# Softmax attention with fp32r row tiles, 1024 wide exponentials and a ring of single maximum banks

## Chip, cores and metric

The kernel runs on one core of a Trainium2 chip. The metric is device time in microseconds (us) of one execution. PE is TensorE (PEld its weight loads), ACT ScalarE, DVE VectorE, POOL GpSimd, SP SyncE.

## What is computed

4096 tokens of 256 features pass a linear attention with a layer norm, then a transformer block: layer norm, 16-head softmax attention (head width 16) with an output projection, and a mixture of 8 experts with the best 2 taken. The change is in the softmax attention and what touches it.

```python
h = _layernorm(x, ln1_g, ln1_b)
q = (h @ Wq).reshape(Bb, Ss, H, Dh)
k = (h @ Wk).reshape(Bb, Ss, H, Dh)
v = (h @ Wv).reshape(Bb, Ss, H, Dh)
scores = jnp.einsum('bqhd,bkhd->bhqk', q, k) / jnp.sqrt(jnp.float32(Dh))
attn = jax.nn.softmax(scores, axis=-1)
ctx = jnp.einsum('bhqk,bkhd->bqhd', attn, v).reshape(Bb, Ss, Dd)
x = x + ctx @ Wo
```

The results have to be close to fp32, so operands of fast matmuls are split into parts.

## The kernel before

`linear_attention` ends with a loop over 8 chunks of 512 tokens (`project`, `split`): Q, K and V are projected in fp32, and Q, K and the difference of two K halves (`k_diff`) are split into three bf16 parts by ACT (L325, L331) and DVE (L423, L435) and stored to DRAM by SP.

`softmax_attention` runs 16 heads x 8 query chunks = 128 chunks. Every chunk has 16 steps, of 2 x 128 keys each. Scores are computed transposed (keys on partitions, 512 queries in the free dimension), as one matmul of 96 rows of parts and 2 rows that subtract the row maximum (`scores`, L683). So the maximum must be known before a chunk's scores: it is found 7 chunks ahead. `diff_unit` (L627) computes q(k1 - k2), ACT takes the Relu (L728), `b_unit` (L636) computes qk2, and one DVE instruction (L797) adds the two and takes the maximum. `finish_max` (L773, L775) makes the two rows, and SP writes them into `q_ring` with two DMAs (`rows`, L534), each from 4 partitions to one.

ACT takes two 512 wide exponentials a step (L741). The low part of each probability is made by DVE in 11 steps of 16 (L804) and by POOL in 5 (L590). `values` (L666) multiplies high and low parts with three parts of V in two column halves of the array, five steps later (`LAG`). ACT copies the sum (L733), PE turns it with fp32 matmuls (L649), DVE divides it. Every engine executes its instructions in the order of its own program and waits for the others on semaphores.

Seven chunks of maxima run before the first scores. `output_projection` collects the heads, turns them, multiplies with Wo and adds x1.

The order of PE in a step is the core of the matter:

```python
scores(t, 0)
if ahead:
    diff_unit(n, t)
scores(t, 1)
if ahead:
    b_unit(n, t)
values(i, par if t >= LAG else par_before, t - LAG)
```

## Time and profile before

| | before |
|---|---|
| median of 3 runs | 4782.31 us (4779.12 to 4784.58) |
| the profiled execution, its own time | 4777.63 us |
| its span | 4775.8 us |
| mean granted TensorE clock | 0.942 |
| busy: PE, DVE, ACT, POOL | 4253.5, 3625.5, 3703.7, 2061.1 us |
| DMA | 176.13 MB |

Busy time is the time in which an engine had an instruction in flight. "Idle before" is the time that it stood before a group's instructions, with the instruction that ended the wait. PEclk is the granted clock as a share of 2.4 GHz. An fp32 matmul is recorded as two.

### The profile page before, as it was taken

How to read it: one execution, taken by the hardware profiler on the slowest of the kernel's cores; microseconds unless marked ns; L12 is line 12 of the kernel's file. 1: busy time of each engine (PE TensorE's matmuls, PEld its weight loads, DVE VectorE, ACT ScalarE, POOL GpSimd, SP SyncE). 2: the span in 40 equal slices, each digit the busy share in tenths (PEclk: the TensorE clock that was granted, in tenths of full speed). 3: DMA queues.
4: the chain of work that ended last, by engine and by line, in shares of the span. 5: the costliest groups of instructions: out<-in, count | busy, mean ns of one | idle time of the engine just before them, and what ended most of it. 6: DMA issues, size and time to landing. Idle time of an engine off the chain costs nothing. (4 is left out here: it accounts for less than half of the span.)

```text
span 4775.8 us, 95820 instructions
## 1 busy us (share of the span) xinstructions
PE 4253.5 (89%) x22137; PEld 1697.9 (36%) x22137; DVE 3625.5 (76%) x7256; ACT 3703.7 (78%) x6958; POOL 2061.1 (43%) x1018
## 2 busy tenths in 40 slices
PE   7569999999999999999999999999999963499991
PEld 4322222222222222222222222222222243499991
DVE  3658898989899889988898998889898863133335
ACT  1347999999999999999999999999999841255551
POOL 0011343434344443434343443434343423788875
PEclk8777999999999999999999999999999985699995
DMA  2231010101001010101011010101010014334433
GB/s 78 101 83 17 0 17 0 17 0 17 5 12 17 0 17 0 17 0 17 0 17 16 2 17 0 17 0 17 0 17 0 0 51 140 123 138 137 137 115 114
DMA packets 105461, 176.13 MB, mean 37 GB/s; under 512 B 16512, under 2 KB 87552, under 8 KB 99072
## 3 DMA queue, kind: packets, MB, share of 16 engines
q1 hardware_dynamic: 86864, 146.17, 11.9%
q0 software_dynamic: 6336, 16.79, 1.1%
q10 hardware_dynamic: 12144, 12.06, 0.7%
q14 instruction: 99, 0.81, 0.1%
q8 instruction: 18, 0.29, 0.0%
HBM read 117.55 MB, written 57.15 MB: 37 GB/s over the span
## 5 line engine op out<-in xcount | busy, mean ns | idle before, releaser
L741 ACT ACTIVATE probs<-s_ps 128x512 f32<-128x512 f32 x4096 | 2430.6, 601 | 213.5 <-PE s_ps L683 161.3
L590 POOL TENSOR_TENSOR probs_low<-probs 128x1024 f16<-128x1024 f32 x640 | 1324.6, 2070 | 2082.9 <-ACT probs L741 2082.9
L804 DVE TENSOR_TENSOR probs_low<-probs 128x1024 f16<-128x1024 f32 x1408 | 1820.5, 1295 | 20.9 <-ACT probs L741 20.7
L797 DVE CUSTOM_DVE_ANT_0 excess<-b_ps,excess 128x512 f32<-128x512 f32 x2048 | 1401.9, 687 | 332.5 <-ACT excess L728 264.7
L683 PE MATMUL s_ps<-q_ring,k_ring 98*128 (+1 forms) x4096 | 1565.1, 384 | 13.8 <-ACT probs L741 8.6
L728 ACT ACTIVATE excess<-diff_ps 128x512 f32<-128x512 f32 x2048 | 1215.4, 594 | 57.9 <-PE diff_ps L627 48.9
L666 PE MATMUL o_ps<-probs,v_parts 128*64 128x512 bf16 x4106 | 854.1, 412 | 74.8 <-ACT o_here L733 72.2
L683 PEld LDWEIGHTS s_ps<-q_ring,k_ring 98*128 98x128 bf16 x4096 | 434.3, 106 | 1160.3 <-ACT probs L741 574.1
L627 PE MATMUL diff_ps<-kd_ring,q_ring 96*128 (+1 forms) x2048 | 801.1, 391 | 50.5 <-issue 38.2
L636 PE MATMUL b_ps<-k_ring,q_ring 96*128 (+1 forms) x2048 | 798.9, 390 | 11.5 <-DVE unit_max L797 10.7
L666 PE MATMUL o_ps<-probs_low,v_parts 128*64 128x512 f16 x4106 | 783.7, 378 | 0.0
L666 PEld LDWEIGHTS o_ps<-probs,v_parts 128*64 128x64 bf16 x4106 | 228.3, 106 | 908.2 <-issue 510.6
L1480 DVE TENSOR_TENSOR hidden_low<-h_ps,hidden_high 128x512 fp32r<-128x512 f32 x184 | 127.2, 691 | 369.8 <-ACT hidden_high L1444 369.8
L1440 ACT ACTIVATE h_ps<-h_ps,b_here 128x512 f32<-128x512 f32 x184 | 121.4, 660 | 261.1 <-PE h_ps L1377 261.0
L636 PEld LDWEIGHTS b_ps<-k_ring,q_ring 96*128 (+1 forms) x2048 | 200.6, 98 | 128.4 <-DVE unit_max L797 61.4
L627 PEld LDWEIGHTS diff_ps<-kd_ring,q_ring 96*128 (+1 forms) x2048 | 201.4, 98 | 98.8 <-issue 93.1
L666 PEld LDWEIGHTS o_ps<-probs_low,v_parts 128*64 128x64 bf16 x4106 | 233.6, 109 | 0.3
L649 PEld LDWEIGHTS misc_ps<-gather,o_here 128*128 128x128 f32 x1032 | 153.2, 188 | 216.4 <-issue 215.2
L1389 PE MATMUL y_ps<-w_low,hidden_high 128*128 128x256 f32 x736 | 209.3, 284 | 0.0
L1389 PE MATMUL y_ps<-w_high,hidden_high 128*128 128x256 f32 x736 | 207.9, 282 | 0.0
L1389 PE MATMUL y_ps<-w_high,hidden_low 128*128 128x256 f32 x736 | 206.7, 281 | 0.0
L649 PE MATMUL misc_ps<-gather,o_here 128*128 128x17 f32 x1032 | 203.6, 273 | 0.7 <-ACT o_here L733 0.7
(195 smaller groups left out, 3445.3 us busy)
## 6 DMA issues: line engine op xcount, KB each, us to landing
w_in<-in_W SPq DMA_DIRECT2D x46, 1024.0 KB, 4.9
q_ring<-qs_dram SPq DMA_DIRECT2D x96, 128.0 KB, 4.4
k_ring<-ks_dram SPq DMA_DIRECT2D x96, 128.0 KB, 7.1
slots_dram<-zero_rows SPq DMA_DIRECT2D x24, 512.0 KB, 6.4
rows_e<-slots_dram SPq DMA_DIRECT2D x24, 512.0 KB, 3.9
y_slots_dram<-y_out ACTq DMA_DIRECT2D x23, 512.0 KB, 4.1
qs_dram<-parts SPq DMA_DIRECT2D x16, 384.0 KB, 3.0
ks_dram<-parts SPq DMA_DIRECT2D x16, 384.0 KB, 4.2
```

What stands on the lines that cost most here:

```text
L590: nc.gpsimd.tensor_tensor(probs_low[:, t % BUFS, :, :], probs[:, t % BUFS, :, :], high[:, :, :, 1], ALU.subtract).then_inc(pool_low_done, 1)
L627: nc.tensor.matmul(diff_ps[:, u % 2, :], q_ring[0:SROWS, ds(q, P)], kd_ring[:, ds(k, CHUNK)], start=True, stop=True).then_inc(diff_done, 1)
L636: nc.tensor.matmul(b_ps[:, u % 2, :], q_ring[0:SROWS, ds(q, P)], keys[:, :, 1, :], start=True, stop=True).then_inc(b_done, 1)
L649: last = nc.tensor.matmul(out_ps[:, t, :], o_here[:, P * t:P * t + P], gather[:, :], start=True, stop=True)
L666: last = nc.tensor.matmul(o_ps[V_COLS * k:V_COLS * k + V_COLS, :], v_parts[:, par, 2 * at + k, :], part[:, k, :], start=(t == 0 and low == ...
L683: nc.tensor.matmul(s2_ps[:, k, :], k_ring[:, col:col + P], q, start=True, stop=True).then_inc(s2_done, 1)
L728: nc.scalar.activation(excess[:, u % 2, :], diff_ps[:, u % 2, :], ACT.Relu).then_inc(excess_ready, 1)
L741: nc.scalar.activation(probs[:, t % BUFS, k, :], s2_ps[:, k, :], ACT.Exp).then_inc(exp_done, 1)
L797: nc.vector.tensor_tensor_reduce(excess[:, u % 2, :], b_ps[:, u % 2, :], excess[:, u % 2, :], 1.0, LEAST, ALU.add, ALU.max, unit_max[:, u ...
L804: nc.vector.tensor_tensor(probs_low[:, t % BUFS, :, :], probs[:, t % BUFS, :, :], high[:, :, :, 1], ALU.subtract).then_inc(low_done, 1)
L1389: last = nc.tensor.matmul(y_ps[:, b, t // 2, D * (t % 2):D * (t % 2) + D], h[:, f % 4, cols], w[:, b, f, :], start=(f == 0 and n == 0 and ...
L1480: nc.vector.tensor_tensor(hidden_low[:, f % 4, :], h_ps[:, f % 2, :], hidden_high[:, f % 4, :].bitcast(F32), ALU.subtract).then_inc(low_do ...
```

## The change

Q and K are split into two fp32r parts in place of three bf16 ones, so a product needs 3 x 16 = 48 rows (50 with the maximum's two). The operands are held twice, at partitions 0 and 64, and two matmuls for two halves of the keys stand side by side in the rows of the array. A slot has one exponential of 1024 columns over both (`s_ps` has two buffers of two banks). Maxima are found two chunks ahead (`LEAD`): in 11 of 16 slots DVE reads both maximum banks by itself, in the 5 of `RELU_PAIRS` the old way with Relu is taken. The maximum banks are a ring of three, `m_ps`, each freed by itself; the turned output takes a turn in it. `finish_max` has four steps, in slots 1, 4, 7 and 10 of the next chunk's maxima, the last a DVE transpose of 32 x 32 blocks, from which SP writes the rows with 16 DMAs (2 row halves x 2 parts x 4 blocks) instead of 2. Probabilities are kept for 16 slots. Five slots of 16 (`FULL_UNITS`) are multiplied in fp32 without a split; the other 11 are split by POOL alone. The visits of P times V stand at the slots of `SLOTS` (those from 16 on fall into the next chunk). Q comes by chunk into four buffers (6 DMAs each); the context goes to DRAM undivided with its sums, two DMAs a chunk, and `output_projection` reads it back, spreads the inverted sums with a matmul per half and scales. The diff, cut to its core:

```diff
-PARTS = 3
...
-Q_PARTS = (0, 0, 0, 1, 1, 2)
-K_PARTS = (0, 1, 2, 0, 1, 0)
...
+PARTS = 2
+Q_PARTS = (0, 0, 1)
+K_PARTS = (0, 1, 0)
...
+TOP_ROW = 64
...
+SIDE = TOKENS // 2
+UNITS = SIDE // P
+KCH = SIDE // CHUNK
+PAIR = 2 * CHUNKS
+RING = HEADS * CHUNKS
+Q_BUFS = 4
+LEAD = 2
+SQ = 32
...
-LAG = 5
-BUFS = 8
...
+ROW_DMAS = 16 * 2 * MROWS * (P // SQ)
+
+FULL_UNITS = (3, 6, 9, 12, 15)
+POOL_UNITS = tuple(t for t in range(UNITS) if t not in FULL_UNITS)
+VISITS = ((0, 1), (3,), (2, 4), (6,), (5, 7), (9,), (8, 10), (12,), (11, 13), (15,), (14,))
+SLOTS = (10, 12, 14, 15, 16, 18, 19, 20, 22, 23, 24)
+COPY_SLOT, TURN_SLOT = 8, 11
+RELU_PAIRS = (1, 4, 7, 10, 14)
+FINISH_SLOTS = (1, 4, 7, 10)
+RING_BLOCKS = 2 * UNITS + 1
+TURN_BLOCK = 2 * TURN_SLOT + 2
...
-                for s in range(5):
-                    act.wait_ge(rest_ready, c * 5 + (s + 6))
-                    nc.scalar.activation(parts[:, b, s, 1, :], rest[:, s, :], ACT.Copy).then_inc(mid_ready, 1)
...
+        q_stage = sb("q_stage", [TOP_ROW + AROWS, Q_BUFS * CHUNK], F32R)
+        k_ring = sb("k_ring", [TOP_ROW + AROWS, 2, SIDE], F32R)
+        kd_ring = sb("kd_ring", [SROWS, 2, SIDE], F32R)
...
+        probs = sb("probs", [P, UNITS, 2, CHUNK])
+        probs_low = sb("probs_low", [P, len(POOL_UNITS), 2, CHUNK], F16)
...
+        excess = sb("excess", [P, CHUNK])
...
+        s_ps = ps("s_ps", [P, 2, 2, CHUNK])
+        m_ps = ps("m_ps", [P, 3, CHUNK])
...
+            def load_q(h, qc, buf):
+                for at in (0, TOP_ROW):
+                    for n, part in enumerate(Q_PARTS):
+                        sp.dma_start(q_stage[at + DH * n:at + DH * n + DH, ds(buf * CHUNK, CHUNK)].bitcast(F32),
...
-                for r in range(MROWS):
-                    sp.dma_start(q_ring[SROWS + r:SROWS + r + 1, ds(col, CHUNK)].rearrange("a (t n) -> a t n", t=TPC),
-                                 max_parts[:, r, :]).then_inc(row_in, 16)
-                sp.wait_ge(row_in, n * (MROWS * 16) + MROWS * 16)
...
+            def rows(n, buf):
+                sp.wait_ge(max_ready, n + 1)
+                for at in (0, TOP_ROW):
+                    for r in range(MROWS):
+                        row = q_stage[at + SROWS + r:at + SROWS + r + 1, ds(buf * CHUNK, CHUNK)].bitcast(F32)
+                        row = row.rearrange("a (t b n) -> a t b n", t=TPC, b=P // SQ)
+                        for b in range(P // SQ):
+                            sp.dma_start(row[:, :, b, :], max_turned[SQ * b:SQ * b + TPC, r, :]).then_inc(rows_in, 16)
...
+                i = sp.snap(h * CHUNKS + qc)
+                if loads:
+                    sp.wait_ge(s_done, i * UNITS + 1)
+                    n = qc + LEAD + 1
+                    load_q(sp.snap(h + n // CHUNKS), n % CHUNKS, n % Q_BUFS)
+                    if more and qc == 0:
+                        load_head(sp.snap(h + 1), sp.snap((h + 1) & 1))
+                if ahead:
+                    rows(i + 1, (qc + 1) % Q_BUFS)
+                if before:
+                    store(i - 1, 1 - qc % 2, sp.snap(h - 1) if qc == 0 else h, (qc - 1) % CHUNKS)
...
+            def max_pair(it, c, t):
+
+                par, buf = c % PAIR // CHUNKS, c % Q_BUFS
+                col = buf * CHUNK + P * (t // KCH)
+                key = CHUNK * (t % KCH)
+                for k, at in enumerate((0, TOP_ROW)):
+                    b = block_of(t, k)
+                    if c * RING_BLOCKS + b > 2:
+                        pe.wait_ge(m_read, it * (PAIR * RING_BLOCKS) + (c * RING_BLOCKS + b - 2))
+                    ring = kd_ring if k == 0 and t in RELU_PAIRS else k_ring
+                    nc.tensor.matmul(m_ps[:, b % 3, :], q_stage[at:at + SROWS, col:col + P],
+                                     ring[at:at + SROWS, par, key:key + CHUNK], start=True, stop=True).then_inc(m_done, 1)
...
+            def scores(it, c, t):
+                par, buf = c % PAIR // CHUNKS, c % Q_BUFS
+                if c * UNITS + t > 1:
+                    pe.wait_ge(exp_done, it * (PAIR * UNITS) + (c * UNITS + t - 1))
+                for k, at in enumerate((0, TOP_ROW)):
+                    last = nc.tensor.matmul(s_ps[:, t % 2, k, :], k_ring[at:at + AROWS, par, P * t:P * t + P],
+                                            q_stage[at:at + AROWS, buf * CHUNK:buf * CHUNK + CHUNK], start=True, stop=True)
...
+                    if t in FULL_UNITS:
+                        for k in range(2):
+                            last = nc.tensor.matmul(o_ps[V_COLS * k:V_COLS * k + V_COLS, :],
+                                                    v_full[:, par, FULL_UNITS.index(t), k, :], probs[:, t, k, :],
+                                                    start=False, stop=False)
+                        continue
+                    for n, part in enumerate((high_view[:, t, :, :, 1], probs_low[:, POOL_UNITS.index(t), :, :])):
+                        for k in range(2):
+                            last = nc.tensor.matmul(o_ps[V_COLS * k:V_COLS * k + V_COLS, :],
+                                                    v_parts[:, par, first_tile(t) + 2 * k, :], part[:, k, :],
+                                                    start=(first and n == 0), stop=(final and n == 1))
...
+            def turn_o(it, c):
+
+                pe.wait_ge(o_copied, it * PAIR + c)
+                pe.wait_ge(m_read, it * (PAIR * RING_BLOCKS) + ((c + LEAD) * RING_BLOCKS + TURN_BLOCK - 2))
+                nc.tensor.matmul(m_ps[:, TURN_BLOCK % 3, :], gather[:, :], o_here[:, :], start=True, stop=True
+                                 ).then_inc(o_turned, 1)
...
+                pe.wait_ge(rows_in, (it * PAIR + (c + 1)) * ROW_DMAS)
+                for t in range(UNITS):
+                    scores(it, c, t)
                     if ahead:
...
+                        max_pair(it, c + LEAD, t)
+                    for visit, slot in enumerate(SLOTS):
+                        if slot == t:
+                            values(it, c, visit)
+                        if slot == t + UNITS and c > 0:
+                            values(it, c - 1, visit)
+                    if t == TURN_SLOT and c > 0:
+                        turn_o(it, c)
...
+            def chunk(i, ahead, first=False):
+                for t in range(UNITS):
+                    if ahead and t in RELU_PAIRS:
+                        excess_pair(i + LEAD, t)
+                    act.wait_ge(s_done, i * UNITS + (t + 1))
+                    if not first:
+                        act.wait_ge(pv_done, i * len(VISITS) + (visit_of(t) + 1 - len(VISITS)))
+                    nc.scalar.activation(probs[:, t, :, :], s_ps[:, t % 2, :, :], ACT.Exp).then_inc(exp_done, 1)
+                    if t == COPY_SLOT and not first:
+                        copy_o(i)
...
+            def pair(n, t, b, skip):
+
+                qt, j = t // KCH, t % KCH
+                if t in RELU_PAIRS:
+                    dve.wait_ge(excess_ready, n * len(RELU_PAIRS) + (RELU_PAIRS.index(t) + 1))
+                    dve.wait_ge(m_done, n * (2 * UNITS) + (2 * t + 2))
+                    dve.sem_inc(dve_passed, 1)
+                    nc.vector.tensor_tensor_reduce(excess[:, :], m_ps[:, block_of(t, 1) % 3, :], excess[:, :], 1.0, LEAST,
+                                                   ALU.add, ALU.max, unit_max[:, b, qt, 2 * j:2 * j + 1]
+                                                   ).then_inc(m_read, 2)
+                    return
+                for k in range(2):
+                    dve.wait_ge(m_done, n * (2 * UNITS) + (2 * t + k + 1))
+                    nc.vector.tensor_reduce(unit_max[:, b, qt, 2 * j + k:2 * j + k + 1], m_ps[:, block_of(t, k) % 3, :],
+                                            AX.X, ALU.max).then_inc(m_read, 1 + skip * k)
...
+                if step == 3:
+                    dve.wait_ge(low_done, n + 1)
+                    nc.vector.transpose(max_turned[:, :, :].rearrange("p r n -> p (r n)"),
+                                        max_parts[:, :, :].bitcast(F32).rearrange("p r n -> p (r n)")).then_inc(max_ready, 1)
...
+            def chunk(n, b, ahead=True, finish=True, turn=True, stores=None):
+
+                for t in range(UNITS):
                     if ahead:
-                        unit(n, t)
-                    if t == LAG + TPC + 3:
-                        finish_max(n)
...
+            def spread(c):
+
+                if c == 0:
+                    pe.wait_ge(z_ready, 1)
+                    pe.wait_ge(picks_made, CHUNKS)
+                if c >= 2:
+                    pe.wait_ge(headsT_ready, 2 * (c - 1))
+                for j in range(HALVES):
+                    heads = of_head[:, c, HEADS // 2 * j:HEADS // 2 * j + HEADS // 2, :].rearrange("p h d -> p (h d)")
+                    last = nc.tensor.matmul(z_ps[:, c % 2, j, :], heads, z_inv[:, :], start=True, stop=True)
...
+            def scale(c):
...
+                for j in range(HALVES):
+                    nc.vector.tensor_tensor(headsT[:, c % 2, j, :], ctxT[:, c, j, :], z_ps[:, c % 2, j, :], ALU.mult
```

## Rows read from the trace of the kernel before

**Rows 1.** Busy time of each engine in a stretch of the main loop (sum 1200 us).

```profile
2400.00:3600.00 1200.00, 1163.55 (x6071) 342.47 (x6069) 1080.67 (x2124) 1131.92 (x2171) 513.66 (x251) 1.00 0.07 9
```

**Rows 2.** The costliest groups of instructions: busy us, mean ns, idle before and releaser.

```profile
L741 ACT ACTIVATE probs<-s_ps 128x512 f32<-128x512 f32 x4096 | 2430.6, 601 | 213.5 <-PE s_ps L683 161.3
L804 DVE TENSOR_TENSOR probs_low<-probs 128x1024 f16<-128x1024 f32 x1408 | 1820.5, 1295 | 20.9 <-ACT probs L741 20.7
...
L1429 ACT ACTIVATE m_high<-mT_e 128x1024 fp32r<-128x1024 f32 x24 | 25.4, 1059 | 0.8
```

**Rows 3.** Single lines of the attention stage: ns min/median/max, first and last start.

```profile
L733 ACT ACTIVATE o_here<-o_ps x19: 592/592/592, 441.1 to 929.3; 128x512 f32<-128x512 f32 x19
...
L741 ACT ACTIVATE probs<-s_ps x4096: 589/597/645, 429.3 to 3859.6; 128x512 f32<-128x512 f32 x196
...
L797 DVE CUSTOM_DVE_ANT_0 excess<-b_ps,excess x2048: 675/685/693, 326.9 to 3713.1; 128x512 f32<-128x512 f32 x187
```

**Rows 4.** Timeline of one chunk: start us, us, engine, line, operation, operands.

```profile
1500.06 0.60 ACT L741 ACTIVATE probs<-s_ps 128x512 f32<-128x512 f32 x1 [0.16 <-PE s_ps L683]
...
1500.08 0.38 PE L683 MATMUL s_ps<-q_ring,k_ring 98*128 x1
...
1500.55 0.59 ACT L728 ACTIVATE excess<-diff_ps 128x512 f32<-128x512 f32 x1
...
1500.60 0.42 PE L666 MATMUL o_ps<-probs,v_parts 128*64 128x512 bf16 x2
...
1500.86 0.38 PE L666 MATMUL o_ps<-probs_low,v_parts 128*64 128x512 f16 x2
...
1501.03 0.60 ACT L741 ACTIVATE probs<-s_ps 128x512 f32<-128x512 f32 x1
...
1501.16 0.40 PE L649 MATMUL misc_ps<-gather,o_here 128*128 128x17 f32 x2
...
1503.09 0.69 DVE L797 CUSTOM_DVE_ANT_0 excess<-b_ps,excess 128x512 f32<-128x512 f32 x1 [1.05 <-ACT excess L728]
...
1503.71 0.08 DVE L797 DVE_READ_ACCUMULATOR2_ANT unit_max<- 128x1 f32 x1
```

**Rows 5.** The POOL split line: ns min/median/max, first and last start.

```profile
L590 POOL TENSOR_TENSOR probs_low<-probs x640: 1892/1895/2875, 439.2 to 3860.4; 128x1024 f16<-128x1024 f32 x160
```

**Rows 6.** SyncE's queue: DMA instructions of two lines, their wait, two in time.

```profile
L534 SPq DMA_DIRECT2D q_ring<-max_parts x270: 595/607/791, 332.3 to 3858.6; - x135
...
L520 SPq DMA_DIRECT2D q_ring<-qs_dram x96: 324/325/953, 302.5 to 3481.3; - x96
...
SPq L537 <- DMA q_ring<-max_parts: 128.9, 135, 1.6
...
1513.43 1.35 SPq L534 DMA_DIRECT2D q_ring<-max_parts  x2
```

**Rows 7.** Stretches of the first phase: busy us of PE, PEld, DVE, ACT, POOL, then PEclk.

```profile
242.00:245.00 3.00, 0.00 (x0) 0.00 (x0) 3.00 (x8) 2.93 (x6) 0.00 (x0) 1.00 0.00 0
245.00:246.00 1.00, 0.82 (x6) 0.82 (x7) 1.00 (x3) 0.30 (x1) 0.00 (x0) 0.82 0.00 0
246.00:249.00 3.00, 3.00 (x10) 2.55 (x9) 2.13 (x4) 1.93 (x3) 0.00 (x0) 0.50 0.75 247
249.00:252.00 3.00, 3.00 (x9) 1.54 (x9) 0.00 (x0) 1.16 (x2) 0.00 (x0) 0.99 1.02 328
```

**Rows 8.** Timeline: fp32 and fp32r matmuls of 512 columns.

```profile
249.52 7.03 PE L270 MATMUL banks<-hT,w_qkv 128*128 128x512 f32 x16
...
4201.13 0.39 PE L1377 MATMUL h_ps<-m_high,w_high 128*128 128x512 f32 x1
...
4201.36 0.40 PE L1377 MATMUL h_ps<-m_low,w_high 128*128 128x512 f32 x1
```

**Rows 9.** Timeline: first instruction of the projection and of the stage behind it.

```profile
3865.93 0.43 SPq L868 DMA_DIRECT2D w_o<-in_Wo  x1
...
3930.98 0.38 SPq L970 DMA_DIRECT2D w_g<-in_Wg  x1
```

More of the change, by code:

```diff
@@ new lines, in _, with chunk @@
+            for i in range(LEAD + 1):
+                load_q(sp.snap(0), i, i)
+            rows(0, 0)
+            def chunk(h, qc, loads=True, more=True, ahead=True, before=True):
+                i = sp.snap(h * CHUNKS + qc)
[9 more added lines that the diff above has]
+                    store(i - 1, 1 - qc % 2, sp.snap(h - 1) if qc == 0 else h, (qc - 1) % CHUNKS)
@@ new lines, in _ @@
+            for qc in range(CHUNKS):
+                chunk(sp.snap(0), qc, before=qc > 0)
+            with sp.Fori(1, HEADS - 1) as h:
+                for qc in range(CHUNKS):
+                    chunk(h, qc)
+            for qc in range(CHUNKS):
+                chunk(sp.snap(HEADS - 1), qc, loads=qc + LEAD + 1 < CHUNKS, more=False, ahead=qc + 1 < CHUNKS)
+            store(RING - 1, 1, sp.snap(HEADS - 1), CHUNKS - 1)
+            for b in range(2):
+                sp.wait_ge(ctx_out[b], 32 * (RING // 2))
@@ L719, in _ @@
+            turn_o(HEADS // 2 - 1, PAIR)
         @block.scalar
@@ L752, in _ @@
+            for n in range(LEAD):
+                for t in RELU_PAIRS:
+                    excess_pair(n, t)
+            chunk(0, True, first=True)
+            with act.Fori(1, RING - LEAD) as i:
+                chunk(i, True)
+            for i in range(RING - LEAD, RING):
+                chunk(i, False)
             copy_o(RING)
@@ L830, in row_statistics @@
+            chunk(RING + 2, 0, ahead=False, finish=False, stores=RING // 2 - 1)
 def row_statistics(nc, dve, ch, stats, mean_var, std, rstd, var_ready, std_ready, n):
```

631 lines of the change are left out of this document (267 added, 364 removed).

## The prediction

> **What bounds the kernel now.** I read the busy time by stretches first, then the groups of instructions, then the timeline of one chunk, and last SyncE's queue. In the main loop [rows 1] ACT is busy 1131.92 of 1200 us, PE 1163.55, DVE 1080.67 and POOL 513.66, at the full granted clock: no engine stands out, POOL is free. Per chunk ACT has 32 exponentials of 512 columns, 16 Relus and a copy [rows 2]; DVE has 11 splits of 1.295 us and 16 fused sums with a maximum, POOL 5 splits. A chunk takes (929.3 - 441.1) / 18 = 27.1 us [rows 3]. The first exponential starts at 429.3 us, and the copy after the last chunk belongs to the projection's start at 3865.9 [rows 3, 9]; the loop with its short last chunks is about 3434 us. What surrounds it is 4777.6 - 3434 = 1344 us of the profiled execution's own time. The median of the three runs is 4.7 us above that time, so the sum needs no correction.
>
> **The engines' sums per chunk after the change.** ACT: 16 exponentials 1024 wide, 5 Relus, a copy. Instructions of 512 columns start 0.49 and 0.48 us apart [rows 4]. A 1024 wide exponential is not in the trace; from below it costs 0.49, from above twice that. The nearest row, a 1024 wide copy at 1059 ns [rows 2] against 601, adds 0.46: I take 0.94 from start to start and 1.04 to its semaphore. Sum 16 x 0.94 + 6 x 0.49 = 18.0 us. DVE: all splits go; 22 single maxima of 512 columns and 5 fused ones. A maximum alone isn't in the trace; the fused one frees DVE after 1503.71 - 1503.09 = 0.62 us and its result is out at 0.70 [rows 4]. Below, 0.49 (ACT's pass over the same 512), above, 0.70; I take 0.62: 27 x 0.62, a copy of 0.62 and 0.8 for the small steps give 18.2 us. POOL: 11 splits, which take 1.895 us where DVE leaves POOL alone and up to 2.875 where not [rows 5]; DVE now reads at most one SBUF tensor. 11 x 1.895 = 20.8 us and per head one split of V (about 7 us, from below 0, from above 11) give 21.7 us a chunk.
> PE: a slot has four fp32r matmuls in two pairs on separate row halves. fp32r of 512 columns starts every 0.23 us [rows 8]. That a row pair runs together is not in the trace; column pairs do, 0.26 us from pair to pair [rows 4]. Below 0.21, above 0.47 a pair; the column pair is nearest, 0.26. An fp32 matmul of 512 columns is 16 records in 7.03 us, two to each, so 0.88 us [rows 8]; I take 0.86 for a full unit's column pair (above 1.72 if its halves run one after the other). From the last column pair to the next matmul 0.30 instead of 0.22 pass [rows 4]: 0.1 us for each change of tiling. 16 x 0.52 + 11 x 0.48 + 5 x 0.86 + 11 visits x 0.2 + 1.0 for the turn = 21.1 us.
> The Trainium skill (TensorE: Matmul & The Clock Gate, Part 3, "Measured speedup vs the span model") has row tiles side by side, 3.07 times for four; by it the pair is as I take it, and no row here shows it. If pairs of fp32r did not overlap, PE would have 16 x 2 x 0.21 = 6.7 us more.
> By sums alone a chunk would take about 22 us. Two things that the sums leave out decide.
>
> **The slots are chained.** The ring of three maximum banks and the single `excess` put PE, ACT and DVE in a row. At a Relu pair the Relu stands ahead of the exponential on ACT and needs the bank that PE fills after its scores; the fused maximum follows it, and frees both banks; the next slot's second maximum matmul waits for that, and the P times V visit is queued behind it. Walked with the durations above: scores of slot 0 at 0, exponential 0 from 0.45 to 1.5, visit ends 1.7; slot 1's bank full at 2.4, Relu to 3.0, maximum to 3.7; slot 2's second bank only then, its visit to 5.0; slot 3 starts at 5.0, slot 4 at 6.7, slot 6 at 9.6, slot 8 at 12.65, slot 10 at 14.45, its Relu behind copy and exponential 9 to 16.3, fused maximum and the fourth finishing step to 17.1 us. On that pace 16 slots take 23.6 us.
>
> **The rows come late.** `finish_max` of chunk i+1 ends after DVE's slot 10 of chunk i. Only then may SP issue that chunk's rows: 2 row halves x 2 parts x 4 blocks = 16 DMAs in place of 2, and PE waits for all 16 ahead of the first scores of chunk i+1. A DMA from four partitions occupies SP for 607 ns, never under 595, where loads of 16 partitions take 325 [rows 6]; two with their address steps take 1.35 us [rows 6], so the gap is from 0 to 0.14; the new addresses are constants, I take 0.05. 16 x 0.607 + 15 x 0.05 = 10.5 us. SP then waited 128.9 us in 135 waits, 0.95 us each, for the rows to land [rows 6]. The other 8 DMAs a chunk (6 loads of Q, 2 stores), and 9 more at a head's start, take 3 to 6 us of SP before slot 10 or after the rows and cost nothing.
> With the walk: 17.1 + 10.5 + 1.0 = 28.6 us, against slots done at 23.6: PE idles about 5 us in each chunk. After an idle stretch of over 3 us the granted clock is 0.82 and then 0.50 (1.2 GHz) over the next 3 us and 0.99 after that [rows 7]. At 1.2 GHz slots 0 and 1 take PE 1.1 and 0.4 us longer (matmuls of 512 columns 0.43 apart instead of 0.22), slot 3 starts at 6.5 and the walk ends 1.5 us later, at 18.6. The period is 18.6 + 10.5 + 0.95 = **30.0 us**, 2.9 more than 27.1.
>
> **The rest.** Before the loop 7 chunks of maxima alone from 326.9 to 429.3 [rows 3] become two, the second up to slot 10, and the first rows: loads until about 320, 20 + 13.5 us of maxima, 11.5 of rows, first exponential at 365: -64 us. In the first phase five copies and five subtractions a chunk go; there PE waits for the normalised rows, which they don't hold up: -5 (0 to -16). DRAM writes grow from 1.9 to 2.5 MB a chunk, beside 16 us of matmuls: 0. The projection took 3930.98 - 3865.93 = 65 us [rows 9]; its transposes and copies are replaced by two fp32 spreading matmuls, PE about 5.2 instead of 5.8 us a chunk, and x1 comes in pieces: -13. The tail after the last exponential (visits, turn, store): +8. Last two chunks without maxima: -15. Sum: 4777.6 - 3434 - 89 + 128 x P = 1254 + 128 P. With P = 30.0: **5100 us**. No change is P = 27.5.
>
> **Rivals.**
> 1. *The walk stalls too much* (faster). If PE, ACT and DVE overlap up to the longest sum, the end of slot 10 is PE's 12.5 us for slots 0 to 9 plus scores, Relu, maximum and step, 14.3 us. P = 25.8, 4550 us; 24.8 to 27.3 over the bounds. It decides from slot 10's end under 16.0 us. For it: before, PE, ACT and DVE run at 90 to 97% of the loop [rows 1]. Against: there DVE and ACT had two buffers each. 25%.
> 2. *The small DMAs are cheap* (faster). At the 325 ns of the loads, 16 take 6 us, rows land by 24.1 us, and the free pace of 23.6 holds, over POOL's 21.7: 4275 us (4030 to 4400). For it: constant addresses. Against: all 270 of this kind took 595 ns or more [rows 6]. 13%. The Trainium skill (DMA: Bandwidth & Descriptors, "Anatomy of one DMA") puts a sequencer's dispatch at some 50 ns; by it 16 would take 0.8 us and this rival would hold; the 607 ns row speaks against it for SP's occupancy.
> 3. *The clock stays at 1.2 GHz* through most of a chunk, or pairs don't overlap. PE then needs 2 x 18 + 2.2 = 38 us a chunk; 33 to 40 by its share: 5480 to 6370, middle 5900 us. For it: idle then dense and sparse slots. Against: at half the clock PE is never idle, and in rows 7 it came back. 13%.
> The forecast (rows late, chained slots) has 47%, with P from 28 to 32.5 and **4840 to 5420 us as its own range**; 2% lie within 0.2% (about 10 us, what a measurement of this kernel can tell from no change). Faster 0.25 + 0.13 = 0.38, slower 0.47 + 0.13 = 0.60. From 4300 to 5550 us leaves out about two thirds of rival 2 and of rival 3, and the ends of the others: 2 in 10.
>
> **What the profile after would show.** Right: about 30 us between the copies of O; SP's row DMAs near 607 ns, 16 in a run of 10 us; PE's wait at a chunk's first scores put down to those DMAs, about 5 us, 126 times, and a clock under full speed behind it; POOL idle several us a chunk; first exponential near 365 us. Wrong: no such wait (rival 2, or a slot pace over 1.9 us), DVE's fourth finishing step less than 16 us after the chunk's start (rival 1), or a clock near 0.5 through whole chunks (rival 3).

## The result, and the profile after

The changed kernel takes 5608.96 us (median of 4 runs, 5577.70 to 5611.69) against 4783.10 us before: ratio 1.1716, interval 1.1679 to 1.1752, so 17% slower. The forecast of 5100 us had the sign and the beginning of the mechanism (rows late, PE idle, clock down), but it was 509 us too low and its range ended at 5550: what the low clock costs was put far too small. The profiled execution took 5611.69 us, its span is 5609.8 us; the terms below are held against that. One of the four executions of experiment e13 took 9637.6 us where the others took 4469.8 to 4473.0; it stands outside that kernel's ratio.

The same stretch of the loop as in [rows 1], by engine:

```profile
core 0: us, PE busy (x) PEld busy (x) DVE busy (x) ACT busy (x) POOL busy (x), PEclk, DMA share, GB/s
2400.00:3600.00 1200.00, 1039.49 (x4576) 394.31 (x4574) 650.36 (x1302) 666.24 (x774) 751.76 (x428) 0.80 0.06 12
```

ACT went from 1131.92 to 666.24 us and DVE from 1080.67 to 650.36. Part of that is only that fewer chunks fit into the stretch: by the chunk (27.1 us before, 34.1 here, see below) ACT went from 25.6 to 18.9 us, DVE from 24.4 to 18.5 and POOL from 11.6 to 21.4, where the forecast had 18.0, 18.2 and 21.7. So the work did move as it was to. PE is still busy 1039 of 1200 us, but at a mean clock of 0.80 where it had 1.00. The steps of 1 us below show the clock at 1.00 or 0.50 but for the steps in which it changes; so a mean of 0.80 is 40% of the time at 0.50.

The copies of O, one a chunk, and SP's row DMAs (groups by tile; ns minimum, median, maximum, then first and last start in us):

```profile
L752 ACT ACTIVATE o_here<-o_ps x128: 592/598/601, 413.8 to 4705.6; 128x512 f32<-128x512 f32 x128
...
L540 SPq DMA_DIRECT2D q_stage<-max_turned x2048: 572/573/771, 356.9 to 4670.5; - x187
```

A chunk takes (4705.6 - 413.8) / 127 = 33.8 us. That mean has the two short chunks at the end in it, which find no maxima; in the middle of the loop the median from one chunk's first scores to the next's is 34.1 us. Before it was 27.1 [rows 3], and 30.0 was forecast.

The costliest groups of the page after, to set beside [rows 2] and [rows 5]:

```profile
L623 POOL TENSOR_TENSOR probs_low<-probs 128x1024 f16<-128x1024 f32 x1408 | 2639.4, 1895 | 1646.9 <-ACT probs L761 1641.3
L761 ACT ACTIVATE probs<-s_ps 128x1024 f32<-128x1024 f32 x2048 | 2071.7, 1024 | 1200.2 <-PE s_ps L673 1197.2
L795 DVE TENSOR_REDUCE unit_max<-m_ps 128x1 f32<-128x512 f32 x2816 | 1810.6, 684 | 1119.0 <-PE m_ps L665 1111.0
L673 PE MATMUL s_ps<-q_stage,k_ring 50*128 50x512 f32 x4096 | 1183.6, 561 | 397.5 <-DMA q_stage<-max_turned 359.9
L789 DVE CUSTOM_DVE_ANT_0 excess<-m_ps,excess 128x512 f32<-128x512 f32 x640 | 442.7, 692 | 874.7 <-ACT excess L748 555.9
```

Every unit price was near its forecast: POOL's split 1895 ns, the 1024 wide exponential 1024, the single maximum 684. ACT, DVE and POOL each wait for something over 1000 us. The fourth row has what they wait for in the end: the scores, and before these the rows.

The timeline from slot 10's maximum to the next chunk's first scores and the transpose after that:

```profile
1508.40 0.69 DVE L789 CUSTOM_DVE_ANT_0 excess<-m_ps,excess 128x512 f32<-128x512 f32 x1 [0.35 <-ACT excess L748]
1509.02 0.24 DVE L822 STREAM_TRANSPOSE max_turned<-max_parts 128x64 f32<-128x64 f32 x1
...
1509.28 9.86 SPq L540 DMA_DIRECT2D q_stage<-max_turned  x16
...
1520.27 0.79 PE L673 MATMUL s_ps<-q_stage,k_ring 50*128 50x512 f32 x2 [3.10 <-DMA q_stage<-max_turned]
...
1543.13 0.24 DVE L822 STREAM_TRANSPOSE max_turned<-max_parts 128x64 f32<-128x64 f32 x1
```

SP starts the 16 DMAs 0.02 us after the transpose ends and is busy 9.86 us with them; PE starts 1.13 us after that, idle for 3.10 us. From the first scores at 1520.27 to the end of the next transpose at 1543.37 pass 23.1 us, where the forecast had 18.6. 23.1 + 9.9 + 1.1 = 34.1 us for this chunk.

The same time in steps of 1 us (columns as above):

```profile
1517.00:1518.00 1.00, 0.16 (x2) 0.00 (x0) 0.47 (x1) 0.07 (x1) 0.87 (x1) 1.00 0.01 1
1518.00:1519.00 1.00, 0.00 (x0) 0.00 (x0) 0.00 (x0) 0.00 (x0) 0.00 (x0) 0.96 0.01 1
1519.00:1520.00 1.00, 0.00 (x0) 0.00 (x0) 0.00 (x0) 0.00 (x0) 0.00 (x0) 0.50 0.01 1
...
1525.00:1526.00 1.00, 0.34 (x1) 0.00 (x0) 0.61 (x1) 1.00 (x3) 0.00 (x0) 0.50 0.00 0
1526.00:1527.00 1.00, 0.85 (x3) 0.42 (x5) 0.81 (x5) 0.95 (x2) 0.89 (x1) 0.50 0.00 0
...
1531.00:1532.00 1.00, 1.00 (x6) 0.23 (x4) 0.32 (x1) 0.00 (x0) 0.00 (x0) 0.50 0.00 0
1532.00:1533.00 1.00, 1.00 (x6) 0.47 (x8) 0.00 (x0) 0.11 (x1) 0.00 (x0) 0.71 0.00 0
1533.00:1534.00 1.00, 1.00 (x6) 0.21 (x3) 0.24 (x1) 1.00 (x2) 0.00 (x0) 1.00 0.00 0
```

The clock falls to 0.50 (1.2 GHz) in the idle stretch and stays there until past 1532, through twelve us after PE has started again. The three waits of PE that matter here:

```profile
PE s_ps L673 <- DMA q_stage<-max_turned: 359.9, 115, 4.9
PE m_ps L665 <- DVE unit_max L789: 106.6, 138, 1.2
PE m_ps L665 <- DVE unit_max L795: 81.2, 261, 0.5
```

So 3.1 us of waiting for the rows in a chunk, 360 us in all, is what the waits show. The larger cost stands in no wait for the rows: it is in the longer slots (experiment e2 sizes it).

### The profile page after: what moved, and what is told of

It is laid out like the page before. It is cut to its first block and busy times, and to the rows that moved or that the text cites. A ratio compares the mean times of both kernels' runs of the same rounds, so it can differ in the third digit from the quotient of the medians.

```text
span 5609.8 us, 80903 instructions
## 1 busy us (share of the span) xinstructions
PE 4634.8 (83%) x21172; PEld 2130.2 (38%) x21172; DVE 2798.5 (50%) x5778; ACT 2805.7 (50%) x3421; POOL 3362.4 (60%) x1877
## 5 line engine op out<-in xcount | busy, mean ns | idle before, releaser
L623 POOL TENSOR_TENSOR probs_low<-probs 128x1024 f16<-128x1024 f32 x1408 | 2639.4, 1895 | 1646.9 <-ACT probs L761 1641.3
L761 ACT ACTIVATE probs<-s_ps 128x1024 f32<-128x1024 f32 x2048 | 2071.7, 1024 | 1200.2 <-PE s_ps L673 1197.2
L795 DVE TENSOR_REDUCE unit_max<-m_ps 128x1 f32<-128x512 f32 x2816 | 1810.6, 684 | 1119.0 <-PE m_ps L665 1111.0
L673 PE MATMUL s_ps<-q_stage,k_ring 50*128 50x512 f32 x4096 | 1183.6, 561 | 397.5 <-DMA q_stage<-max_turned 359.9
L665 PE MATMUL m_ps<-k_ring,q_stage 48*128 48x512 f32 x3456 | 1273.5, 491 | 213.4 <-DVE unit_max L789 106.6
L673 PEld LDWEIGHTS s_ps<-q_stage,k_ring 50*128 50x128 f32 x4096 | 459.0, 218 | 1562.5 <-issue 1217.6
L789 DVE CUSTOM_DVE_ANT_0 excess<-m_ps,excess 128x512 f32<-128x512 f32 x640 | 442.7, 692 | 874.7 <-ACT excess L748 555.9
L665 PEld LDWEIGHTS m_ps<-k_ring,q_stage 48*128 48x128 f32 x3456 | 625.9, 226 | 614.9 <-DVE unit_max L789 307.3
L690 PE MATMUL o_ps<-probs,v_full 128*64 128x512 f32 x2560 | 803.1, 710 | 0.0
L748 ACT ACTIVATE excess<-m_ps 128x512 f32<-128x512 f32 x640 | 380.8, 595 | 752.3 <-PE m_ps L665 751.9
```

The source lines that it names most:

```text
L623: nc.gpsimd.tensor_tensor(probs_low[:, POOL_UNITS.index(t), :, :], probs[:, t, :, :], high_view[:, t, :, :, 1], ALU.subtract).then_inc(poo ...
L665: nc.tensor.matmul(m_ps[:, b % 3, :], q_stage[at:at + SROWS, col:col + P], ring[at:at + SROWS, par, key:key + CHUNK], start=True, stop=Tru ...
L673: last = nc.tensor.matmul(s_ps[:, t % 2, k, :], k_ring[at:at + AROWS, par, P * t:P * t + P], q_stage[at:at + AROWS, buf * CHUNK:buf * CHUN ...
L690: last = nc.tensor.matmul(o_ps[V_COLS * k:V_COLS * k + V_COLS, :], v_full[:, par, FULL_UNITS.index(t), k, :], probs[:, t, k, :], start=Fal ...
L748: nc.scalar.activation(excess[:, :], m_ps[:, block_of(t, 0) % 3, :], ACT.Relu).then_inc(excess_ready, 1)
L761: nc.scalar.activation(probs[:, t, :, :], s_ps[:, t % 2, :, :], ACT.Exp).then_inc(exp_done, 1)
```

## Experiments

The theory was: rows late, PE idle, clock down, slots longer, rows late again. Rival A: the clock falls because the slots are too sparse, wait or no wait. Rival B: the ring of maximum banks with its Relus sets the pace whatever the clock does. The table has, for the profiled run of each kernel, the mean time from copy of O to copy of O over the whole loop, the mean granted clock from 1600 to 2800 us, and PE's waits for the row DMAs divided by 127 chunks; then the median time of the kernel's executions. Each ratio is to the kernel before, measured beside it: median 4783.1 us beside the changed kernel, 4773.0 to 4774.4 beside the experiments that have a ratio. "One run" is a single execution.

| kernel | us a chunk | clock | row wait, us | time, us | ratio to before |
|---|---|---|---|---|---|
| changed kernel | 33.8 | 0.80 | 2.8 | 5609.0 | 1.1716 (1.1679 to 1.1752) |
| e1 steps at slots 0 to 3 | 27.1 | 0.96 | 0 | 4756.0 | 0.9968 (0.9953 to 0.9983) |
| e2 PE kept busy, rows late | 30.8 | 0.98 | 0 | 5222.6 | one run |
| e3 e1, visits in groups | 27.6 | 0.95 | 0 | 4803.1 | 1.0066 (1.0049 to 1.0083) |
| e4 e1, Relu behind | 31.7 | 0.90 | 0 | 5338.0 | 1.1193 (1.1172 to 1.1214) |
| e5 steps at 1, 3, 5, 7 | 27.0 | 0.96 | 0 | 4736.1 | one run |
| e6 e1, no Relu pairs | 26.9 | 0.96 | 0 | 4710.2 | 0.9862 (0.9845 to 0.9879) |
| e7 no Relu pairs, late | 33.6 | 0.83 | 2.6 | 5570.3 | one run |
| e8 last step after slot 9 | 30.4 | 0.91 | 1.9 | 5168.7 | one run |
| e9 e1, steps as reductions | 27.3 | 0.95 | 0 | 4762.4 | 0.9971 (0.9959 to 0.9983) |
| e10 e9, 15 visits | 26.9 | 0.97 | 0 | 4721.0 | 0.9883 (0.9865 to 0.9901) |
| e11 e10, no Relu pairs | 23.9 | 0.99 | 0 | 4331.6 | 0.9081 (0.9066 to 0.9096) |
| e12 e11, late | 30.8 | 0.83 | 3.0 | 5213.0 | one run |
| e13 e9, no Relu pairs | 25.0 | 0.99 | 0 | 4472.2 | 0.9366 (0.9347 to 0.9384) |
| e14 e13, late | 31.4 | 0.86 | 3.0 | 5294.3 | one run |

**e1: the rows in time.** The only edit:

```diff
-FINISH_SLOTS = (1, 4, 7, 10)
+FINISH_SLOTS = (0, 1, 2, 3)
```

> The changed kernel with the four finishing steps of the row maxima after slots 0 to 3 instead of 1, 4, 7, 10; nothing else moved. Theory (rows land late, PE idles about 3 us, the clock falls, the walk to slot 10 runs at half clock, and so the rows are late again): SP starts the 16 DMAs by 8 us of a chunk, they are in by 19 us, no wait for rows, granted clock above 0.95, chunk 23.6 to 25 us, 4280 to 4450 us in all. Rival A (the clock falls without any wait, because the slots of narrow fp32r tiles are too sparse): no wait for rows, but the clock stays near 0.8 and a chunk takes 29 us or more, 4950 us up. Rival B (the ring of maximum banks, Relu and fused maximum alone set the pace): clock above 0.95 and still 28 us or more, 4850 us up.

The loop's stretch (columns as above), then the first scores of two chunks in a row, between which the clock is full:

```profile
1600.00:2800.00 1200.00, 1114.38 (x5674) 428.66 (x5674) 828.50 (x1613) 825.85 (x960) 932.00 (x534) 0.96 0.08 15
```

```profile
1532.32 0.50 PE L673 MATMUL s_ps<-q_stage,k_ring 50*128 50x512 f32 x2
...
1558.63 0.50 PE L673 MATMUL s_ps<-q_stage,k_ring 50*128 50x512 f32 x2
```

853 us came back and rival A fell: with no wait for rows the clock of the loop is 0.96. The pace that the forecast had for the slots fell too: 27.1 us a chunk, not 23.6 to 25, and 4756.0 us, not 4280 to 4450. In the chunk shown, wholly at full clock, the 16 slots take 26.3 us. Rival B, which asked for 28 us or more, has part of the truth: something other than the rows holds the slots well over the 22 us of the engines' sums. So the change, rows apart, is worth 0.3%, and that comes from outside the loop: in its middle a chunk takes 27.4 us here and 27.1 in the kernel before, while the first exponential starts at 360.1 us instead of 429.3.

**e2: the rows late, the clock up.** 36 matmuls ahead of the wait for the rows:

```diff
+                if c > 0:
+                    pe.wait_ge(exp_done, it * (PAIR * UNITS) + (c * UNITS - 1))
...
+                    for _ in range(FILLERS):
+                        for k, at in enumerate((0, TOP_ROW)):
+                            nc.tensor.matmul(s_ps[:, 0, k, :], k_ring[at:at + SROWS, at_head, 0:P],
+                                             q_stage[at:at + SROWS, at_q:at_q + CHUNK], start=True, stop=True)
```

> The changed kernel with 36 matmuls (18 pairs of 48 rows by 512 columns, results overwritten unused) just ahead of PE's wait for the rows, so that PE is kept busy while they are late; results as before. The rows are as late as ever after slot 10. Theory: the clock stays above 0.95, slot 10 ends near 17 to 18 us, 9.9 us of DMAs and 1 us behind it give 28 to 29 us a chunk, 4850 to 4950 us. Rival A (sparse slots let the clock fall): clock still near 0.8, 33 to 35 us a chunk, 5500 us or more. If the idle time itself and not the clock were the cost: no gain either, 5600 us.

The loop's stretch, then its timeline from one chunk's row DMAs to the next chunk's transpose:

```profile
1600.00:2800.00 1200.00, 1124.98 (x6428) 514.13 (x6422) 708.50 (x1426) 729.63 (x849) 828.20 (x475) 0.98 0.07 14
```

```profile
1501.60 9.86 SPq L541 DMA_DIRECT2D q_stage<-max_turned  x16
...
1509.43 4.39 PE L718 MATMUL s_ps<-q_stage,k_ring 48*128 48x512 f32 x36
1513.65 0.40 PE L674 MATMUL s_ps<-q_stage,k_ring 50*128 50x512 f32 x2
...
1531.76 0.24 DVE L830 STREAM_TRANSPOSE max_turned<-max_parts 128x64 f32<-128x64 f32 x1
```

The rows' DMAs still start only after slot 10, PE does 4.4 us of useless work, and the kernel is 386 us faster than the changed one. The walk from the first scores to the end of the transpose is 1532.00 - 1513.65 = 18.35 us instead of 23.1: in these chunks the clock alone costs 4.75 us. The means say a little less: 33.8 - 30.8 = 3.0 us, and the 1.1 us by which the useless matmuls outlast the rows' landing, so 4.1. The chunk came out 2 us above the expected 28 to 29, and the time at 5222.6 us instead of 4850 to 4950, because of these 1.1 us (scores 2.2 us after the last DMA instead of 1.1), because the walk is 18.35, not 17 to 18, and because some chunks lost about 1.5 us more to a fall of the clock elsewhere. This run is the nearest to the clock's price by itself.

**e8: a little less late.** The last step after slot 9:

```diff
-FINISH_SLOTS = (1, 4, 7, 10)
+FINISH_SLOTS = (1, 4, 7, 9)
```

> The changed kernel with its last finishing step after slot 9 instead of 10 (1, 4, 7, 9). At full clock slot 9 ends 15.8 to 16.5 us into a chunk, so the rows are in about 0.5 to 1.2 us after PE is done with the 16 slots. If the loss grows evenly with lateness: chunk 27.5 to 28 us, 4800 to 4870 us. If the clock makes it feed on itself (a short idle stretch lets the clock fall, the walk gets longer, the idle stretch with it): 30 us or more, 5120 us up.

30.4 us: the second. The waits are shorter and the clock of the loop is still 0.91; PE's wait for the rows in it:

```profile
PE s_ps L673 <- DMA q_stage<-max_turned: 240.4, 114, 3.7
```

With 240.4 / 114 = 2.1 us of idle time the chunk is 3.3 us longer than in e1; the rows' DMAs start one slot earlier than in the changed kernel and the chunk is 3.4 us shorter. Lateness is paid more than once.

**e5: early enough.** `FINISH_SLOTS = (1, 3, 5, 7)`.

> The changed kernel with the finishing steps after slots 1, 3, 5, 7. With the clock up the last of them ends 14.2 us into a chunk, the rows are in by 25.1 us, and the slots take 26.3 us at full clock: theory (only a real wait for rows costs) says no wait and a chunk of about 27.1 us, within 1 per cent of the kernel with steps at 0 to 3, 4710 to 4810 us. If the 16 DMAs themselves or their place beside other loads cost, more than 4850 us.

27.0 us, one wait of 1.0 us in the whole run. The 16 DMAs a chunk, 2048 in all, cost nothing that shows once they end in time.

**e3: the spread of the visits** over the slots, on e1.

```diff
-SLOTS = (10, 12, 14, 15, 16, 18, 19, 20, 22, 23, 24)
+SLOTS = (10, 11, 14, 15, 16, 17, 20, 21, 22, 23, 24)
```

> As the kernel with the finishing steps at slots 0 to 3, but with the P times V visits at slots 10, 11, 14 to 17, 20 to 24 in place of 10, 12, 14, 15, 16, 18, 19, 20, 22, 23, 24: slots 2 and 3 (18 and 19), and 12 and 13, come without a visit, two in a row. Theory: once the rows are in time the spread is worth little, clock above 0.9, within 2 per cent of the kernel with the spread. Rival A (what PE lacks in two slots in a row drops the clock): mean clock under 0.85 and at least 10 per cent slower than with the spread.

4803.1 against 4756.0 us: the spread gives 1.0%, and the clock is the same to 0.01. It is worth little and does not decide the result.

**e4: ACT takes the Relu behind the exponential.**

```diff
-                    if ahead and t in RELU_PAIRS:
-                        excess_pair(i + LEAD, t)
                     act.wait_ge(s_done, i * UNITS + (t + 1))
...
                     nc.scalar.activation(probs[:, t, :, :], s_ps[:, t % 2, :, :], ACT.Exp).then_inc(exp_done, 1)
+                    if ahead and t in RELU_PAIRS:
+                        excess_pair(i + LEAD, t)
```

> As the kernel with the finishing steps at slots 0 to 3, but ACT takes each Relu of the maxima behind the slot's exponential instead of ahead of it. If the chain of PE, Relu and fused maximum sets the pace of a slot, the exponential starts earlier, the fused maximum about 1 us later, and the chunk changes by over 2 per cent either way; the walk has the maximum's end as the link, so about 0.5 us lost at each of 5 Relus, 2.5 us a chunk, 4650 us. If PE's own work sets it, the same time within 1 per cent.

4.6 us a chunk lost, nearly twice the 2.5 of the walk. The chain bank, Relu, fused maximum, bank is real: PE's waits for the fused maximum rose from 153.6 us in e1 to 463.9 us. That is 2.4 us a chunk, as the walk had it; the clock of the loop also fell from 0.96 to 0.90, so the rest lies in slower slots, at least in part.

**e6 and e7: no Relu pairs**, rows early and late.

```diff
-RELU_PAIRS = (1, 4, 7, 10, 14)
+RELU_PAIRS = ()
```

> As the kernel with the finishing steps at slots 0 to 3, and no pair of banks goes by ACT's Relu and the fused maximum: DVE takes all 32 single maxima of a chunk, ACT the 16 exponentials alone. Result as before. If the chain of bank, Relu and fused maximum is what holds the 16 slots at 26.3 us, where PE's own work is about 22 us: chunk 22.5 to 24.5 us (DVE's sum 32 x 0.62 + 1.8 = 21.6, POOL's 21.7), clock near 1.0, 4180 to 4420 us. If something else holds them (PE's gaps between tilings, POOL): 26 us or more, 4650 us up.

> The changed kernel with its late finishing steps (slots 1, 4, 7, 10) but no Relu pair. Theory: PE still idles for the rows and the clock still falls, but with no stall behind a Relu at slot 1 it comes back sooner (4 to 7 us at 1.2 GHz instead of 13); slot 10 ends 3 to 6 us earlier, chunk 28 to 31 us, 4850 to 5250 us. Rival (the time at 1.2 GHz is set by the idle stretch alone): again 13 us of each chunk at half clock, 31 to 33 us, 5250 to 5500 us.

The theory missed in both. In e6 the other case came true (26 us or more, 4650 us up), and e7 lies above even its rival's 31 to 33 us. With the chain gone 26.9 and 33.6 us stay, 0.2 us less than with it. What took its place was found in the steps that write 4 numbers a partition. e6, DVE's finishing steps as groups, then DVE and POOL on the timeline, then the clock behind it:

```profile
L813 DVE SCALAR_TENSOR_TENSOR max_parts<-tile_max,no_max x128: 150/1846/1865, 343.7 to 3779.8; 128x4 fp32r<-128x4 f32 x128
L817 DVE SCALAR_TENSOR_TENSOR max_parts<-tile_max,max_parts x128: 146/730/936, 345.0 to 3780.0; 128x4 fp32r<-128x4 f32 x128
```

```profile
1547.34 5.60 POOL L623 TENSOR_TENSOR probs_low<-probs 128x1024 f16<-128x1024 f32 x3 [0.95 <-ACT probs L761]
...
1549.25 1.86 DVE L813 SCALAR_TENSOR_TENSOR max_parts<-tile_max,no_max 128x4 fp32r<-128x4 f32 x1
...
1551.76 0.72 PE L665 MATMUL m_ps<-k_ring,q_stage 48*128 48x512 f32 x1 [0.80 <-DVE unit_max L795]
...
1552.22 0.73 DVE L817 SCALAR_TENSOR_TENSOR max_parts<-tile_max,max_parts 128x4 fp32r<-128x4 f32 x1
```

```profile
1550.00:1551.00 1.00, 0.96 (x5) 0.30 (x3) 1.00 (x1) 0.15 (x1) 1.00 (x1) 1.00 0.20 66
1551.00:1552.00 1.00, 0.24 (x1) 0.22 (x1) 1.00 (x3) 0.87 (x1) 1.00 (x2) 0.93 0.10 33
1552.00:1553.00 1.00, 1.00 (x5) 0.34 (x6) 1.00 (x3) 0.00 (x0) 0.94 (x1) 0.50 0.00 0
```

POOL's three splits end near 1549.2, 1551.1 and 1552.9. L813 begins with the second and ends with it (1551.11); L817 ends with the third (1552.95). Both read two operands from SBUF. PE then waits 0.80 us for a bank, and the clock falls behind that. In e7 both steps took 1.4 to 1.6 us (median 1577 ns each), and in the chunk at 2420 us the clock fell a second time near 2442, behind such a step; from 1600 to 2800 us it fell 51 times in 35 chunks. The first of the two steps in the changed kernel and in e7:

```profile
L813 DVE SCALAR_TENSOR_TENSOR max_parts<-tile_max,no_max x128: 156/157/164, 348.7 to 4660.6; 128x4 fp32r<-128x4 f32 x128
...
L813 DVE SCALAR_TENSOR_TENSOR max_parts<-tile_max,no_max x128: 149/1577/1594, 343.6 to 4623.6; 128x4 fp32r<-128x4 f32 x128
```

The place in the program is the same, and POOL is busy 750 and 755 of 1200 us. What differs is the moment: a split of POOL was running at the step's start once in 128 times in the changed kernel, and 126 times in 128 in e7.

**e9: the steps without a second SBUF operand.** On e1, with `tile_max` kept as a third row of `max_parts`:

```diff
-                    nc.vector.scalar_tensor_tensor(max_parts[:, 0, 0:TPC], tile_max[:, :], -1.0, no_max[:, :],
-                                                   ALU.mult, ALU.add).then_inc(high_done, 1)
+                    nc.vector.tensor_reduce(max_parts[:, 0, 0:TPC], unit_max[:, b, :, :], AX.X, ALU.max, negate=True).then_inc(high_done, 1)
...
-                    nc.vector.scalar_tensor_tensor(max_parts[:, 1, 0:TPC], tile_max[:, :], -1.0,
-                                                   max_parts[:, 0, 0:TPC].bitcast(F32), ALU.mult, ALU.subtract
-                                                   ).then_inc(low_done, 1)
+                        nc.vector.tensor_reduce(max_parts[:, 1, 0:TPC],
+                                                max_parts[:, 0:MROWS + 1:MROWS, 0:TPC].bitcast(F32).rearrange("p r t -> p t r"),
+                                                AX.X, ALU.add, negate=True).then_inc(low_done, 1)
```

> As the kernel with the finishing steps at slots 0 to 3, with finishing steps 1 and 2 as reductions with a negated result in place of two operations with two SBUF operands each; same result. In that kernel the second of them took 733 ns in the middle of 128 and up to 1164, the first up to 1895, ends falling on the ends of POOL's splits, 157 ns where POOL was idle. If that wait for POOL, with PE idle 1.2 us behind it and the clock at 1.2 GHz for 3.5 us after that, is what lies between 27.1 us and the 26.3 us of a chunk wholly at full clock: no such step over 250 ns, granted clock of the loop above 0.98, 26.2 to 26.6 us a chunk, 4640 to 4690 us. If the block costs nothing on the path: 4740 to 4770 us as before.

The steps are down to 181 and 151 ns (longest 188 and 161), so the wait for POOL is gone, and the time is that of e1, as the expectation's second case had it. Its timeline behind slot 1:

```profile
1539.77 0.08 DVE L789 DVE_READ_ACCUMULATOR2_ANT unit_max<- 128x1 f32 x1
...
1539.90 0.49 PE L665 MATMUL m_ps<-k_ring,q_stage 48*128 48x512 f32 x1 [1.20 <-DVE unit_max L789]
...
1541.74 0.79 PE L673 MATMUL s_ps<-q_stage,k_ring 50*128 50x512 f32 x2
```

The Relu pair of slot 1 holds PE 1.20 us by itself, and the clock falls behind it (0.50 from 1541 to 1544). PE's waits for the fused maxima are what they were, 152.7 us against 153.6 in e1, so DVE's wait for POOL must have lain beside them in e1; that last step is inferred.

**e10, e11, e13: the slots without a visit.** In e6 a slot without a visit takes 0.58 us and the one behind it 2.37 (scores at 1541.00, 1541.58, 1543.95), where a slot with a visit of the same size takes 1.67: PE must wait until DVE has read a bank. 15 visits in place of 11 leave one such slot instead of five (e10 has this on top of e9):

```diff
-VISITS = ((0, 1), (3,), (2, 4), (6,), (5, 7), (9,), (8, 10), (12,), (11, 13), (15,), (14,))
-SLOTS = (10, 12, 14, 15, 16, 18, 19, 20, 22, 23, 24)
+VISITS = ((0, 1), (2,), (3,), (4,), (5,), (6,), (7,), (8,), (9,), (10,), (11,), (12,), (13,), (15,), (14,))
+SLOTS = tuple(range(10, 25))
```

> The same, and the P times V work in 15 visits at slots 10 to 24, one tile each but for the first of two, in place of 11 visits of one or two tiles with 5 slots without any. If the ring of three banks holds PE to DVE's pace of 1.25 us a slot, so that the time of a slot without a visit (0.57 us) is lost again in the next (2.4 instead of 1.67): slots of 1.22 us (one tile) and 1.67 (a full unit or two tiles), PE's sum 9 x 1.22 + 6 x 1.67 + 1.0 + 0.6 + 0.7 = 23.3, a chunk 23.3 to 24.8 us, 4270 to 4470 us. If the visits' number only adds 0.1 us each and nothing was lost in the short slots: 26.5 us or more, 4680 us up.

> The same with 15 visits, and no Relu pairs (DVE takes all 32 single maxima of a chunk). Without the Relu chain, but with DVE at 32 x 0.62 + 1.8 = 21.6 us: between 23 and 24.5 us a chunk if PE's sum holds, 4230 to 4430 us; if DVE's pace with three banks holds it, slower than with the Relu pairs by up to 1 us a chunk.

> Finishing steps at slots 0 to 3 as single-operand reductions, no Relu pairs, and the 11 visits of the changed kernel. Between the kernel without Relu pairs (26.9 us a chunk) and the one that also has 15 visits and the reductions (23.9) two things differ; this one has the reductions alone. If the visits' spread makes the difference (a slot without a visit takes 0.57 us and the next then 2.37 instead of 1.67, five times a chunk, as the ring of three banks holds PE to DVE's pace): 25.5 to 26.4 us a chunk, 4540 to 4650 us. If DVE's wait for POOL in the finishing steps made it (1.85 and 0.73 us a chunk, and the clock's fall behind it): 23.9 to 24.8 us, 4330 to 4450 us.

e10, with the Relu pairs, gained 0.4 us of the 2.5 to 4 expected: a slot with a Relu pair and one tile takes 2.56 us there (scores at 1506.86 and 1509.42). e11, without the Relu pairs, gained 3.4 us over e9: 23.9 us a chunk and 4331.6 us, 9.2% under the kernel before, as it was put ahead of the run (4230 to 4430). e13 splits what lies between e6 and e11: 26.9 to 25.0 is DVE's wait for POOL with what hangs on it, 25.0 to 23.9 the spread of the visits. It fell between the two forecasts, since both were right in part. Three stalls stood one behind another. Against e1, the Relus removed alone gave 0.2 us (e6) and the wait for POOL alone nothing (e9); Relus and wait for POOL together gave 2.1 us (e13), all three 3.2 (e11). The spread of the visits was never run alone; with the wait for POOL it gave 0.2 (e10).

The loop of e11 (columns as above):

```profile
1600.00:2800.00 1200.00, 1186.56 (x6479) 464.02 (x6478) 1042.12 (x1844) 829.63 (x847) 1060.98 (x609) 0.99 0.09 17
```

PE is busy 1186.56 of 1200 us at 0.99 of the clock, so what a chunk waits for now is nearly all PE's own work. The forecast's sum for it, 21.1 us and 4 more visits at 0.2, is 2 us short of the 23.9.

**e12 and e14: the fast kernels with their rows late again**, `FINISH_SLOTS = (1, 4, 7, 10)` in e11 and in e13.

> As the kernel with 15 visits and no Relu pairs (23.9 us a chunk), but the finishing steps back after slots 1, 4, 7 and 10, as in the changed kernel. At full clock slot 10 would end 15.8 us into a chunk; with 9.9 us of DMAs and 1 us to land that is 26.7, so PE idles about 3 us again. Theory (the idle stretch lets the clock fall, and the slots up to the tenth then take 4 to 5 us longer): 30.5 to 32 us a chunk, 5180 to 5370 us, granted clock of the loop near 0.8. If a kernel whose PE is busy without gaps gets its clock back within 3 to 4 us: 27.5 to 28.5 us, 4800 to 4930 us. Each is well above the 4332 us of the kernel with early steps.

> The same with the finishing steps after slots 1, 4, 7 and 10, as in the changed kernel. The kernel without Relu pairs and late took 33.6 us a chunk, with two finishing steps held 1.4 to 1.6 us by POOL and the clock falling a second time near slot 10. If those waits kept the clock down: no second fall, no step over 250 ns, 29.5 to 31.5 us a chunk, 5050 to 5310 us. If an idle stretch of 3 us for the rows alone costs 12 us or more at 1.2 GHz whatever follows: 32.5 us or more, 5430 us up.

30.8 us for e12, as expected: 6.9 us a chunk and 881 us in all for the place of four short instructions. e14 came out as expected too. Without DVE's waits for POOL it has 38 falls of the clock in the 38 chunks from 1600 to 2800 us, where e7 had 51 in 35, and 31.4 us instead of 33.6; in the chunk at 1530 us the clock is at 0.50 until 1536 and full again from 1537. A mean clock of 0.80, 0.83 and 0.86 means 13.5, 10.5 and 8.8 us a chunk at 1.2 GHz in the changed kernel, e12 and e14 (twice the missing share times the chunk), at nearly the same mean wait of 3.1, 3.3 and 3.3 us (359.9 / 115, 380.6 / 115, 374.8 / 114). What sets that length was not found.

## Why the forecast was wrong in size

By its own steps, the term 1254 + 128 P first (with P = 30.0 it is 5094 us, given as 5100). P is a chunk in the middle of the loop, and that was 34.1 us instead of 30.0, which is 128 x 4.1 = 525 us. The surroundings were 5609.8 - 128 x 34.1 = 1245 instead of 1254. In them the first exponential came at 368.9 (365 forecast), and the last two chunks, without maxima, took 20.7 and 18.5 us; they saved 29 us, not 15. So the whole miss is P, and P fails in the walk.

- **Rows late, 16 DMAs ahead of PE's wait.** Right. 16 x 0.607 + 15 x 0.05 = 10.5 us forecast, 9.86 measured (573 ns each, a median of 2048), and 1.13 to PE's start where 0.95 was put. PE's idle stretch was 3.1 us, not 5, and came 115 times, not 126, because the slots that it follows took longer too. The Trainium skill's 50 ns for a dispatch (DMA: Bandwidth & Descriptors, "Anatomy of one DMA"), which the forecast set against the 607 ns row, stands there for DMAs on GpSimd's path, and it does not describe how long SP is held here (573 ns). Rival 2 fell. Its sum had a slip besides: rows that land at 24.1 us come after the pace of 23.6, so its period was 24.1 us and its time 4339 us, not 4275.
- **The chained slots.** Right in kind, short in size. "the fourth finishing step to 17.1 us", and 16 slots in 23.6: at full clock it is 18.35 (e2) and 26.3 us (e1). The walk had slots 3, 8 and 10 start at 5.0, 12.65 and 14.45 us; in e1 they start 5.5, 13.5 and 15.75 us after slot 0. Slot 6 alone, behind slot 5 that has no visit, took 2.17 us there, and the walk had both slots 6 and 7 in 3.05.
- **The clock.** This is the step that failed: "At 1.2 GHz slots 0 and 1 take PE 1.1 and 0.4 us longer [...] and the walk ends 1.5 us later, at 18.6". It took [rows 7], where the clock is back 3 us after an idle stretch, for the rule. There PE went from idle to one dense run of matmuls; here the slots of the chain follow, and the clock stayed at 0.50 for 12 us after PE's start. That this difference is the reason was not tested. The walk became 23.1 - 18.35 = 4.75 us longer, not 1.5. The two misses of the walk, 1.25 and 3.25, less 0.4 on the DMAs and their landing, give the 4.1 us by which P was missed.
- **Rival 3**, "the clock stays at 1.2 GHz through most of a chunk", had 13% and P from 33 to 40. Its mechanism came true in part: 13.5 of 33.8 us at half clock, and a time inside its 5480 to 6370. The reason against it, that PE at half clock is never idle, was wrong: in the changed kernel PE idles 3.1 us and 40% of the time still goes by at half clock. The two cases were not rivals but one mechanism, the forecast's idle stretch being what starts rival 3 anew in every chunk. The Trainium skill (TensorE: Matmul & The Clock Gate, "HAM oscillation — how this bites in real kernels") describes just that, a wait for a DMA in each round after which each round starts at the half clock; e1 against the changed kernel agrees, 0.96 and 0.80.
- **Rival 1** (an end of slot 10 under 16.0 us) fell with 18.35 us at full clock.
- **POOL's splits at 1.895 us** held everywhere (1893 to 1895). The forecast's "DVE now reads at most one SBUF tensor" left out the two finishing steps, which read two. In the changed kernel that cost nothing (median 157 ns, 164 at most), because in 127 of 128 chunks POOL stood idle when the first of them came, and in all 128 when the second came. That was luck of the timing: in e7, as late and with POOL as busy, both steps waited.
- **Pairs of row tiles** run side by side, as taken: two matmuls of 512 columns in 0.50 us, the next pair 0.34 later.
